# The 16 columns of negated row maxima per half, turned by one transpose into 16 partitions

## The reference, cut to what matters

```
q  = layernorm(x).reshape(B, 8, 32, 512)       # k and v come from the context in the same way
qk = einsum('bhdq,bhdl->bhql', q, k) * 32**-0.5
sm = softmax(qk, axis=-1)                      # over the 512 keys
x  = x + gamma * einsum('bhql,bhdl->bhdq', sm, v)
```

## Time and profile before

| what | value |
|---|---|
| median of 3 executions | 1885.12 us (1884.68 to 1885.8) |
| the profiled execution's own time | 1885.63 us |
| its span, first to last instruction | 1883.7 us |
| granted clock of PE, mean | 0.952 |
| PE busy | 1669.9 us, 89% of the span |
| DVE busy | 1229.2 us, 65% |
| ACT busy | 1008.3 us, 54% |
| POOL busy | 950.4 us, 50% |

### The profile page before, as it was taken

How to read it: one execution, slowest core, us unless ns; L and a number is a source line. 1 busy time by engine, 2 the same in 40 slices (tenths; PEclk the granted TensorE clock), 3 DMA queues, 4 the chain that set the end, 5 groups by cost and what they waited for, 6 DMA issues and landing times.

```text
span 1883.7 us, 26169 instructions
## 1 busy us (share of the span) xinstructions
PE 1669.9 (89%) x8672; PEld 1079.5 (57%) x8672; DVE 1229.2 (65%) x2708; ACT 1008.3 (54%) x1970; POOL 950.4 (50%) x880
## 2 busy tenths in 40 slices
PE   4688999999999999999999997836999999999995
PEld 2344445445545445445545543325998888888884
DVE  2364676776776776776776776433776666666662
ACT  3235556556556556556556554513665555555552
POOL 1112224364364364364364363655676666766665
PEclk9779999999999999999999998967999999999998
DMA  9786423443443443432432321026999999999995
GB/s 339 218 279 220 117 57 110 138 157 109 139 156 109 126 142 99 111 112 79 106 88 67 87 59 46 25 83 200 259 261 247 255 249 262 252 247 242 256 252 82
DMA packets 138196, 303.32 MB, mean 161 GB/s; under 512 B 26617, under 2 KB 27513, under 8 KB 138062
## 3 DMA queue, kind: packets, MB, share of 16 engines
q1 hardware_dynamic: 99150, 230.23, 40.4%
q0 software_dynamic: 38912, 71.43, 16.8%
HBM read 132.60 MB, written 155.91 MB: 153 GB/s over the span
## 4 chain that ended last, share of the span: by engine, by line
PE 38%; DMA 21%; issue 13%; POOL 12%; DVE 10%; ACT 3%; SPq 3%; POOLq 0%; ACTq 0%; DVEq 0%
DMA out_rows<-y_slots,row_ids 19%; POOL slot_rows L1423 5%; PE bank L663 5%; PE bank L655 4%; PE bank L636 4%; PE bank L676 4%; POOL p_sum L1411 3%; PE bank L699 3%; SPq L414 2%; POOL out_rows L1472 2%; PE bank L609 2%; PE bank L577 2%; DVE max_col L1185 2%; PE bank L623 1%; PE bank L692 1%
## 5 line engine op out<-in xcount | busy, mean ns | idle before, releaser
L1185 DVE TENSOR_REDUCE max_col<-bank 128x1 f32<-128x512 f32 x512 | 345.2, 683 | 216.6 <-PE bank L655 214.1
L940 ACT ACTIVATE p_t<-bank 128x512 f32<-128x512 f32 x512 | 298.1, 597 | 283.2 <-PE bank L663 263.1
L1423 POOL DMA_INDIRECT slot_rows<-row,slot_i x256 | 267.8, 1046 | 329.9 <-DVE slot_i L1284 261.3
L1472 POOL DMA_INDIRECT out_rows<-y_slots,row_ids x128 | 228.2, 1783 | 197.2 <-DMA out_rows<-y_slots,row_ids 148.2
L663 PE MATMUL bank<-q_stack,k_stack 98*128 98x512 f32 x512 | 275.4, 539 | 5.4 <-ACT p_t L940 5.1
L655 PE MATMUL bank<-k_stack,q_stack 96*128 96x512 f32 x512 | 216.2, 424 | 19.2 <-DMA q_stack<-xn 16.3
L1411 POOL TENSOR_TENSOR p_sum<-p_t 128x512 f32<-128x512 f32 x128 | 162.5, 1277 | 139.4 <-ACT p_t L940 138.3
L1462 POOL TENSOR_TENSOR down_lo<-down,down_hi 96x1024 fp32r<-96x1024 f32 x64 | 188.4, 2944 | 16.1 <-DVE down_hi L1347 16.0
L784 PE MATMUL bank<-gate_up_hi,x_slots_t_hi 128*128 128x384 f32 x512 | 186.4, 364 | 0.5 <-DVE x_slots_t_lo L1316 0.5
L1316 DVE TENSOR_TENSOR x_slots_t_lo<-bank,x_slots_t_hi 128x512 fp32r<-128x512 f32 x128 | 88.2, 689 | 142.5 <-ACT x_slots_t_hi L999 142.5
L785 PE MATMUL bank<-gate_up_lo,x_slots_t_hi 128*128 128x384 f32 x512 | 175.0, 342 | 0.0
(11 more groups left out here) (175 smaller groups left out, 3342.0 us busy)
## 6 DMA issues: line engine op xcount, KB each, us to landing
gate_up<-in_gate_up SPq DMA_DIRECT2D x64, 768.0 KB, 6.4
slot_rows<-row SPq DMA_DIRECT2D x64, 577.0 KB, 8.0
x_slots<-slot_rows SPq DMA_DIRECT2D x64, 577.0 KB, 4.6
k_stack<-prob SPq DMA_DIRECT2D x192, 128.0 KB, 2.4
down<-in_down SPq DMA_DIRECT2D x64, 384.0 KB, 7.3
q_stack<-x_t SPq DMA_DIRECT2D x128, 128.0 KB, 2.3
x<-in_x SPq DMA_DIRECT2D x16, 512.0 KB, 4.2
ctx<-in_ctx SPq DMA_DIRECT2D x16, 512.0 KB, 3.8
```

Source lines behind the costliest of these rows:

```text
L940: e.activation(p_t[step % 2][:, h, :], psum[n % 2][:, :], ACT.Exp, scale=SCALE).then_inc(free[n % 2], 1)
L1185: e.tensor_reduce(max_col[quad % 2][:, c, h:h + 1], psum[2 + n % 2][:, :], X, ALU.max, negate=True).then_inc(free[2 + n % 2], 1)
L1423: e.indirect_dma_start(out=slots_dram, in_=rows[b % 2][:, k, :], in_offset=None, out_offset=bass.IndirectOffsetOnAxis(ap=slot_i[b % 2][:, ...
L1472: e.indirect_dma_start(out=out, out_offset=bass.IndirectOffsetOnAxis(ap=row_ids[e_ % NI][:, q, :].bitcast(U32), axis=0), in_=ye[e_ % NY][: ...
```

## The change

`max_col` is laid out as heads by blocks, so that its 16 columns are one run. One transpose turns all of them into 16 partitions x 128 queries (partition `h * 4 + c`). `max_hi` and `max_lo` become 16 x 128 tiles. Each of the two DMAs reads 16 partitions of 512 bytes and writes them side by side into the same 8 KB of its row of the query stack, where before it read 4 partitions of 2 KB.

```diff
-        max_col = [A(f"max_col{i}", [P, C, H4]) for i in range(2)]
-        max_hi = A("max_hi", [H4, T], F32R)
-        max_lo = A("max_lo", [H4, T], F32R)
+        max_col = [A(f"max_col{i}", [P, H4, C]) for i in range(2)]
+        max_hi = A("max_hi", [H4 * C, P], F32R)
+        max_lo = A("max_lo", [H4 * C, P], F32R)
@@ SP, max_rows
-                    e.dma_start(q_st[b % 2][row:row + 1, heads, :].bitcast(F32),
-                                part[:, :].bitcast(F32)).then_inc(max_in, 16)
+                    dst = q_st[b % 2][row:row + 1, heads, :].rearrange("o h (c q) -> o (h c) q", q=P)
+                    e.dma_start(dst.bitcast(F32), part[:, :].bitcast(F32)).then_inc(max_in, 16)
@@ PE, finish_quad "max"
-                    for c in range(C):
-                        m = e.transpose(bank[0:H4, c * P:(c + 1) * P], max_col[quad % 2][:, c, :], ident[:, :])
-                    m.then_inc(done, 1)
+                    cols = max_col[quad % 2][:, :, :].rearrange("p h c -> p (h c)")
+                    e.transpose(bank[0:H4 * C, 0:P], cols, ident[:, :]).then_inc(done, 1)
@@ ACT, finish_quad "max"
-                    e.copy(max_hi[:, :], bank[0:H4, :]).then_inc(max_hi_ok, 1)
+                    e.copy(max_hi[:, :], bank[0:H4 * C, 0:P]).then_inc(max_hi_ok, 1)
@@ DVE, score_chunk
-                e.tensor_reduce(max_col[quad % 2][:, c, h:h + 1], psum[2 + n % 2][:, :], X, ALU.max,
+                e.tensor_reduce(max_col[quad % 2][:, h, c:c + 1], psum[2 + n % 2][:, :], X, ALU.max,
                                 negate=True).then_inc(free[2 + n % 2], 1)
@@ DVE, finish_quad "max_lo"
-                    e.tensor_tensor(max_lo[:, :], bank[0:H4, :], max_hi[:, :].bitcast(F32), ALU.subtract).then_inc(done, 1)
+                    e.tensor_tensor(max_lo[:, :], bank[0:H4 * C, 0:P], max_hi[:, :].bitcast(F32), ALU.subtract).then_inc(done, 1)
```

## The result

| | before | after |
|---|---|---|
| median of 20 executions each | 1884.71 us (1880.2 to 1890.31) | 1889.67 us (1882.9 to 1898.13) |
| ratio after to before | | 1.003, 95% interval 1.0018 to 1.0042 |
| the profiled execution's own time | 1885.63 us | 1883.75 us |
| its span; mean granted clock | 1883.7 us; 0.952 | 1882.0 us; 0.957 |
| PE, DVE, ACT busy | 1669.9, 1229.2, 1008.3 us | 1655.1, 1205.9, 999.0 us |

The kernel became slower by 0.3%, some 5 us. (Two executions of the experiments, 3279 us of `e3_four_transposes` and 7354 us of before on its chip, count in no ratio.) I had forecast 2.5 us less. The one profiled execution of after happens to be a good one, so its span can't be read against that of before. The first phase and the expert phase have to be taken apart. The first expert matmul starts at 1287.9 us before and at 1291.98 after: the first phase is 4.1 us longer.

A forecast was written before the change was run, and what follows sets the result against it. It took a settled batch to be bound by a chain of waits through PE, ACT, POOL and DVE, not by PE alone; 1.0 + 0.3 + 1.2 = 2.5 us saved gave a median of 1882.6 us, range 1875.0 to 1886.0.

The forecast's parts named there:

- Worth 0: PE, odd halves at L577 and settled even halves at L609: the 0.33 us saved per half becomes idle time, gaining 0.
- SP and the DMAs: Two DMAs per half in 16 pieces of 512 bytes should issue and land as fast as in 4; cost 0.
- five cases: The forecast (chance 0.52) and its rivals B (0.16), C (0.12), D (0.10) and E (0.10).
- E: Rival: SP's issue or the landing grows with the pieces, so odd halves' key chunks wait; about 1898 us, chance 0.10.
- The four halves on the chain: Transposes of halves 0, 2, 4 and the last lie on PE's chain: 1.0 us together plus 0.3 for half 0.
- ACT and DVE: At each half's maxima, a shorter copy saves 0.29 us and a shorter subtraction 0.38, together 0.67 us per half.
- 0.1 us per batch: POOL's first addition starts 0.1 us sooner, held by ACT's exponential, in twelve batches: 1.2 us, bounds 0 and 8.0.
- B: Rival: DVE's path counts, so each of 12 batches gains the full 0.67 us; 9.3 us in all, 1875.8 us, chance 0.16.
- C: Rival: PE is the bound after all, so all 10.6 us of transposes come back; 1874.5 us, chance 0.12.
- D: Rival: nothing; gains at halves 0, 2, 4 and 31 vanish in later waits, the 0.1 us too; 1885.1 us, chance 0.10.
- The expert phase neither gains nor loses: The phase after the first one, which the change does not touch, only starts sooner; no gain or loss of its own.

The follow-up runs named there:

- e3_four_transposes: The changed kernel with its one transpose issued four times into four parts of the same bank; 1.0001 of the kernel before.
- e7_filled_waits: The changed kernel with useless transposes put into PE's known waits (odd halves, L609, stacks of batches 1, 2, 3 and 15); 1.0019 of the kernel before.
- e8_four_and_two_fills: `e3_four_transposes` plus 20 and 30 useless transposes ahead of the waits for the stacks of batches 1 and 15; 1.0003 of the kernel before.
- e9_one_and_two_fills: The changed kernel plus 20 and 30 useless transposes ahead of the waits for the stacks of batches 1 and 15; 1.0002 of the kernel before.
- r2_after: The changed kernel run again without any edit, as control on another chip; 1.0043 of the kernel before.
- e2_dma_16_only: The kernel before, but its two DMAs per half read a constant tile of zeros in 16 pieces; 1.001 of the kernel before.
- e4_wide_copies: The changed kernel with ACT's copy and DVE's subtraction again over all 512 columns of the bank; 1.0051 of the kernel before.
- e1_dma_4: The changed kernel, but its two DMAs per half read a constant tile of zeros in 4 pieces; 1.0033 of the kernel before.
- e6_even_four: The changed kernel with four transposes at the even halves and one at the odd ones; 1.0004 of the kernel before.

## Why the prediction was wrong

**The step that failed** is in the part on PE: "Shorter transposes lengthen that second idle time from 0.53 to 0.86. Worth 0", and at the even halves "The 0.33 us moves into that idle time. Worth 0". Where the time would go was right to a hundredth (0.85 and 1.26 us). That the move is worth nothing was wrong: it should have stood at about +5 us over the first phase. `e3_four_transposes` shows that this step alone makes the difference (1.0034 with one transposition, 1.0001 with four, on the same chip, all else equal). What the runs showed in place of "worth 0" is a loss outside the settled batches: the stack's DMAs land later in batches 3 and 7, PE waits longer in batches 3, 7 and 15, and it is granted the lower level for longer behind these waits. Which of the two costs how much stays open. I read the granted clock of the settled stretch, 1.00, and had half 0's transposes "at the lower clock" in front of me, and took the clock as given instead of as something that the change can move. In its part on SP and the DMAs the sum asked only what the two DMAs of the maxima would do, not when the stack's would land. None of my five cases had it; the slower one, E, was another mechanism.

That the clock is a link between the change and the time rests on the traces: 0.72 to 0.81 behind the stack of batch 3 in all five traces with one transposition and 1.00 in the four with four; the mean clocks, 0.9463 for after and 0.9505 for `e3_four_transposes`; and batch 15's wait for the stack, where filling it raises the clock from 0.83 to 0.94. It isn't closed: three of the five traces with some 2.3 us at L609 of batch 15 fall there as well, the long waits of batches 3 and 7 go with a late stack, and the gains of `e7_filled_waits` and `e8_four_and_two_fills` in clock bring no time.

On this the Trainium skill has a rule, TensorE: Matmul & The Clock Gate, "Why this matters for your kernels": to avoid drops of throughput in mid-kernel, leave no long PE-idle gaps between bursts of matmuls. The traces agree in direction, and go further: the gaps that the page warns of are longer than the 2.3 to 2.6 us here, behind which the lower level stood. It is the page that I should have weighed against "worth 0".

The same page, "Part 4: PE-mode transpose", holds that a transposition "doesn't count as PE-busy the same way" for the clock. The runs speak against this: with 30 transposes in batch 15's wait the granted clock from 1140 to 1170 us is 0.94, without them 0.83 (`e9_one_and_two_fills` and `r2_after`), and the mean clock rose with transposes alone from 0.9463 to 0.9505 (`e3_four_transposes`) and from 0.9507 to 0.9556 (`e9_one_and_two_fills`).

**The other steps.**
- *The four halves on the chain, 1.3 us:* not found. From POOL's L1390 (one less in after) of batch 0 to that of batch 2, with three of the halves on the way, after takes 136.9 us and before 139.9, but `e3_four_transposes` takes 137.0 with all four transposes and `e2_dma_16_only` 137.0 too. Between batches 2 and 3 after wins 1.5 us more (68.8 for 70.4), where before has the fall at 231 us and after has none. Between batches 3 and 4 all of it is given back (75.8 for 71.7), with the fall at 298 us. A fall was moved, not removed, and met a longer wait for the stack's DMA. Half 0's share can't be read at all: L609 of batch 1 starts at 112.9 to 116.6 us over all traces, in no order of the transposes.
- *ACT and DVE, 0.67 us per half:* the sizes were right, and "not 0.67" too. The 0.1 us per batch (1.2 us in all) didn't come. I let POOL's sends start 0.67 us sooner and cut the gain at ACT's exponential; DVE itself had already lost it, waiting 0.71 us for PE's scores. `e4_wide_copies`, with the 0.6 us given back, agrees: its settled batch is 70.5 us too.
- *SP and the DMAs, 0:* right. 0.56 and 0.69 us for an issue of 16 pieces in half 11, no key chunk that waits for them but in half 0. E is refuted, by `e1_dma_4` too.
- *The rivals:* B and C called for a batch of 69.8 us; it is 70.49. D, nothing, was nearest, and lacked the sign.
- *"The expert phase neither gains nor loses":* its scatter of 16 us from trace to trace is more than all terms of my sum.

## What to carry to other kernels

Where PE is nearly always busy but waits now and then, don't book work taken from PE in front of such a wait at zero: look up the longest waits of a pipeline's start and end, add what the change takes away, and read the granted clock behind them, before and after. Read too when the DMAs land for which PE waits, and whether an instruction load falls among their issues: a change in the number of instructions moves it. Where a wait can't be shortened, transposes that nobody needs inside it held the clock here, as long as they sat where PE would be idle anyway; elsewhere they cost their full time. A filler also moves the instruction loads, so it is no clean test of the wait alone. And when medians differ by 0.3% with one good profile among them, compare the phases and many executions, not the spans of two profiles.

## What the hardware showed that I had not expected

- The granted clock falls in the midst of a stretch in which PE is busy 93% of the time (941.7 of 1010 us in after), behind waits of 1.4 to 2.6 us (0.72 to 0.81 from 292 to 310 us in the kernels with one transposition).
- Not each such wait costs it, and like waits can go either way: behind 2.31 us at L609 the clock of `e6_even_four` fell and behind 2.32 that of `e3_four_transposes` did not.
- A 16 KB instruction load on q8 that starts among 12 DMA issues of SP stretches them from some 7.6 to 8.14 to 9.33 us, in 16 of 16 cases; in after one issue takes 1.64 us for 0.60.
- A chip's own level differs more than any edit here: before takes 1884.7 us on one and 1902.2 on another, the latter at a mean clock of 0.9500, and at 0.9543 on two where it takes 1889 us.
- A DMA of 8 KB into one partition costs SP the same in 16 pieces of 512 bytes as in 4 of 2 KB: 0.56 to 0.69 us to issue.
